# First cross attention of a perceiver block: the context turned by VectorE in 32x32 blocks, six batches ahead, and carried by the DMA of the probabilities

## The reference, cut to what matters

```python
xn, ln_lat = layer_norm(ctx, g1, b1), layer_norm(layernorm(x), g2, b2)
q, kv = ln_lat @ Wq, concat([xn, ln_lat], axis=1) @ Wkv      # 16 heads of 64
w = softmax(where(mask, einsum('bhld,bhnd->bhln', q * s, k * s), neg))
x = x + einsum('bhln,bhnd->bhld', w, v) @ Wout
```

## Time and profile before

| | |
|---|---|
| median of three runs | 2055.35 us (2054.4 to 2057.96) |
| the profiled execution | 2053.8 us, span 2051.7 us |
| busy, share of the span | PE 84%, DVE 78%, ACT 73%, POOL 44% |
| hardware DMA queue | 194678 packets, 256.53 MB, 50.0% of 16 engines |
| mean granted TensorE clock | 0.914 of full speed |

### The profile page before, as it was taken

The page is one execution under the profiler, slowest core; times in us unless marked ns, Lnnn a source line. Parts: engine busy times, 40 slices in busy tenths (PEclk is TensorE's granted clock), DMA queues, the critical chain, the costliest instruction groups (busy, mean ns, idle before and its releaser), DMA issues. The chain is left out here.

```text
span 2051.7 us, 51500 instructions
## 1 busy us (share of the span) xinstructions
PE 1718.3 (84%) x13455; PEld 1392.9 (68%) x13455; DVE 1594.6 (78%) x4998; ACT 1504.4 (73%) x4156; POOL 908.9 (44%) x1339
## 2 busy tenths in 40 slices
PE   3599999999999999971710679999999799749997
PEld 3489999999999999941500356666667566427775
DVE  4798888888888888837788669999999588636664
ACT  3488888888888888854765479999999588545553
POOL 1544444444444444304156034444444377335554
PEclk8599999999999999995755799999999799879998
DMA  4277676777777777610000059999999300103322
GB/s 139 85 167 165 160 160 157 161 163 162 159 162 163 159 160 164 151 42 0 0 0 0 2 147 250 252 250 251 249 249 248 73 1 0 32 13 102 91 87 82
DMA packets 196234, 259.54 MB, mean 127 GB/s; under 512 B 25136, under 2 KB 141328, under 8 KB 196032
## 3 DMA queue, kind: packets, MB, share of 16 engines
q1 hardware_dynamic: 194678, 256.53, 50.0%
q10 hardware_dynamic: 1194, 1.58, 0.3%
q0 software_dynamic: 288, 0.56, 0.1%
HBM read 86.09 MB, written 4.72 MB: 44 GB/s over the span
## 5 line engine op out<-in xcount | busy, mean ns | idle before, releaser
L778 ACT ACTIVATE a_prob<-a_neg,a_nmax 128x289 f32<-128x289 f32 x512 | 266.6, 525 | 1.4 <-DVE a_nmax L705 1.1
L840 PE MATMUL a_out<-a_probT,a_xn 128*128 128x256 f32 x1024 | 263.0, 380 | 5.0 <-DMA a_probT<-a_blocks 4.2
L1710 ACT ACTIVATE b_prob<-b_neg,b_nmax 128x257 f32<-128x257 f32 x512 | 260.6, 515 | 6.9 <-DVE b_nmax L1661 6.8
L671 POOL TENSOR_TENSOR a_xn<-a_z,g 128x256 f32<-128x256 f32 x128 | 93.8, 733 | 384.6 <-DVE a_z L739 384.6
L830 PE MATMUL a_score<-a_xnT,a_qT 128*128 128x290 f32 x1536 | 252.9, 314 | 2.5 <-DVE a_qT L750 2.5
L705 DVE CUSTOM_DVE_ANT_0 a_neg<-a_score,a_bias 128x289 f32<-128x289 f32 x512 | 211.6, 458 | 41.2 <-PE a_score L830 36.8
L786 ACT ACTIVATE a_prob<-a_prob,a_rinv 128x289 f32<-128x289 f32 x512 | 231.3, 527 | 1.8 <-DVE a_rinv L755 1.7
L830 PEld LDWEIGHTS a_score<-a_xnT,a_qT 128*128 128x128 f32 x1536 | 222.3, 190 | 9.6 <-issue 3.3
L1661 DVE CUSTOM_DVE_ANT_0 b_neg<-b_score,b_bias 128x257 f32<-128x257 f32 x512 | 188.6, 419 | 30.5 <-PE b_score L1801 15.3
L840 PEld LDWEIGHTS a_out<-a_probT,a_xn 128*128 128x128 f32 x1024 | 175.2, 191 | 19.8 <-DMA a_probT<-a_blocks 5.3
L716 DVE STREAM_TRANSPOSE a_blocks<-a_prob 128x1024 f32<-128x1024 f32 x128 | 159.4, 1245 | 24.0 <-ACT a_prob L786 17.7
(11 more groups left out here) (478 smaller groups left out, 4567.9 us busy)
## 6 DMA issues: line engine op xcount, KB each, us to landing
a_probT<-a_blocks SPq DMA_DIRECT2D x512, 192.0 KB, 3.6
b_probT<-b_blocks SPq DMA_DIRECT2D x256, 256.0 KB, 4.6
a_raw<-in_ctx SPq DMA_DIRECT2D x128, 128.0 KB, 2.9
b_raw<-in_ctx SPq DMA_DIRECT2D x64, 256.0 KB, 4.7
m_wide<-expert_weights SPq DMA_DIRECT2D x128, 128.0 KB, 2.9
a_kept<-keep SPq DMA_DIRECT2D x32, 257.0 KB, 3.4
b_kept<-keep SPq DMA_DIRECT2D x32, 257.0 KB, 4.8
b_v_rows<-ctx_tail_values SPq DMA_DIRECT2D x32, 256.0 KB, 4.7
```

The costliest lines, as they stand in the source:

```text
L778: nc.scalar.activation(prob[:, par, grp, 0:KEYS0], neg[:, grp, :], ACT.Exp, bias=nmax[:, par, grp:grp + 1], scale=-1.0, accum_out=rsum[:, ...
L840: nc.tensor.matmul(out_ps[:, half, 0:2 * P], xn[:, j, kt, :], probT[:, u, 2 * half:2 * half + 2, kt, :], start=(kt == 0), stop=False)
L1710: nc.scalar.activation(prob[:, (j + 5) % 4, grp, :], neg[:, par, grp, :], ACT.Exp, bias=nmax[:, par, grp:grp + 1], scale=-1.0, accum_out=r ...
```

## The change

The context is no longer transposed by TensorE through PSUM. VectorE turns the normalised context of batch s + 6 in 32x32 blocks into 64 more columns of `blocks`; the four DMAs of the step carry 448 columns instead of 384 and so put it, by features, next to the probabilities. Two steps later (batch s + 4) ScalarE copies it out of `probT` as the high half, and GpSimd subtracts for the low half. The pipeline begins with step -8 instead of -7, and 16 batches instead of 8 lie outside the loop. On TensorE the first values move ahead of queries and projection; on VectorE the statistics go first and the residual add ahead of the queries; ScalarE puts the query copy between exponentials 2 and 3; the projection has a bank of its own; z is written straight into `xn`.

```diff
-        z = sb("a_z", [P, 2, 2, D])
-        blocks = sb("a_blocks", [P, 2, KEY_STEP, KEY_TILES, GROUPS, L])
-        probT = sb("a_probT", [P, 2, 4, KEY_TILES, P])
+        blocks = sb("a_blocks", [P, 2, KEY_STEP, KEY_TILES * P + 2 * L])
+        probT = sb("a_probT", [P, 2, 4, KEY_TILES * P + 2 * L])
-        proj_ps = ctx_ps[:, 2 * P:2 * P + D]
+        proj_ps = proj_bank[:, 0:D]
-        LEAD, LAG = 7, 1
+        LEAD, LAG, REST = 8, 1, 16
-            return (g * 4 + (j // 2 + 1)) * 64
+            return (g * 4 + (j // 2 + 3)) * 64
+        def carried_ctx(j):
+            return probT[:, j % 2, :, KEY_TILES * P:].rearrange("p i (k m) -> p k i m", k=2 * KEY_STEP)
+        def ctx_cols(j, half):
+            return xnT[:, half, (j + 4) % 8, 0:2 * P].rearrange("p (k i m) -> p k i m", k=2 * KEY_STEP, i=4)
...
                 def spread_prob(g, j):
-                    wait_apart(k, sp, blocks_ready, s + 3)
+                    wait_apart(k, sp, blocks_ready, s + 7)
+                    if live(g, j, 4):
+                        wait_apart(k, sp, xnT_ready, s + 5)
...
-                        heads = slice(i * L, (i + 1) * L)
-                        sp.dma_start(probT[:, n, i].rearrange("p t q -> p (t q)"),
-                                     blocks[heads, n].rearrange("c r t g l -> c r (t g l)")).then_inc(probT_loaded[n], 16)
+                        sp.dma_start(probT[:, n, i], blocks[i * L:(i + 1) * L, n]).then_inc(probT_loaded[n], 16)
...
-                    if live(g, j, 8):
-                        if live(g, j, 4):
-                            wait_apart(k, sp, z_ready, s + 5)
-                        load_raw(g + 1, j)
+                    if live(g, j, 9):
+                        if live(g, j, 5):
+                            wait_apart(k, sp, z_ready, s + 6)
+                        load_raw(s + 9, j + 1)
...
             def _(pool):
+                    if live(g, j, 4):
+                        wait_apart(k, pool, xnT_hi, s + 5)
+                        nc.gpsimd.tensor_tensor(ctx_cols(j, LO), carried_ctx(j), ctx_cols(j, HI), ALU.subtract).then_inc(xnT_ready, 1)
...
             def _(dve):
-                    if live(g, j, 0):
+                    if live(g, j, 4) or live(g, j, 2):
...
+                    if live(g, j, 6):
+                        dve.wait_ge(xn_ready, s + 7)
+                        last = nc.vector.transpose(blocks[:, n, :, KEY_TILES * P:].rearrange("p f (r t m) -> p t f m r", r=KEY_STEP, t=2),
+                                                   xn[:, (j + 6) % 8].rearrange("p t (c f) -> p t f c", f=KEY_STEP))
+                    if live(g, j, 2):
+                        dve.wait_ge(prob_ready, s + 3)
+                        nc.vector.transpose(blocks[:, n, 0:2, 2 * P:3 * P].rearrange("p r (g l) -> p g r l", l=L),
+                                            prob[:, n, :, 2 * P:2 * P + 2 * L].rearrange("p g (r c) -> p g r c", c=L))
+                        last = nc.vector.transpose(blocks[:, n, :, 0:2 * P].rearrange("p r (t g l) -> p g r t l", t=2, l=L),
+                                                   prob[:, n, :, 0:2 * P].rearrange("p g (r t c) -> p g r t c", t=2, c=L))
+                    last.then_inc(blocks_ready, 1)
...
+                        wait(dve, out_ready, s)
+                        dve.wait_ge(rstd_ready, s + 8)
...
-                    if live(g, j, 5):
-                        dve.wait_ge(xnT_hi, s + 6)
-                        n = (j + 5) % 8
-                        nc.vector.tensor_tensor(xnT[:, LO, n, 0:2 * P], ctx_ps[:, 0:2 * P], xnT[:, HI, n, 0:2 * P],
-                                                ALU.subtract).then_inc(xnT_ready, 1)
...
+                    if live(g, j, 4):
+                        act.wait_ge(probT_loaded[j % 2], probT_loads(g, j))
+                        nc.scalar.activation(ctx_cols(j, HI), carried_ctx(j), ACT.Copy).then_inc(xnT_hi, 1)
...
-                    if live(g, j, 3):
-                        for grp in range(GROUPS):
-                            exp(g, j, grp)
+                    exps(g, j, (0, 1))
...
-                    if live(g, j, 5):
-                        act.wait_ge(ctx_turned, s + 6)
-                        nc.scalar.activation(xnT[:, HI, (j + 5) % 8, 0:2 * P], ctx_ps[:, 0:2 * P], ACT.Copy).then_inc(xnT_hi, 1)
+                    exps(g, j, (2, 3))
...
+                    if here:
+                        values(g, j, 0)
...
-                        wait(pe, xnT_ready, s + 5 if live(g, j, 4) else B)
+                        wait(pe, x_added, t - 1)
...
-                        values(g, j, 0)
-                    if live(g, j, 5):
-                        n = (j + 5) % 8
-                        pe.wait_ge(xn_ready, s + 6)
-                        wait(pe, xnT_ready, s + 5)
-                        if b == 0:
-                            wait(pe, x_added, t)
-                        for kt in range(2):
-                            last = nc.tensor.transpose(key_order(ctx_ps[:, 0:2 * P], kt), xn[:, n, kt, :], k.ident[:])
-                        last.then_inc(ctx_turned, 1)
```

## The result

The changed kernel takes 2124.59 us (median of four runs, 2121.12 to 2131.56) against 2056.65 us (four runs, 2054.4 to 2058.51) for the kernel before in the same session: a ratio of 1.0335, interval 1.0305 to 1.0365. It is slower by 68 us, beyond the range and beyond all three rivals' times. The profiled execution took 2131.56 us, with a span of 2129.8, against 2053.8 for the one before.

The account below looks back on a forecast made before the run. TensorE, never pausing, was taken as the bound at 24.86 us a tile. -13.5 over 30 tiles and +2.5 outside the body make -11.0: 2053.8 becomes 2042.8, 2044 for the median; range 2031 to 2060, the forecast's own 2037 to 2050.

Parts of the forecast that it names:

- the stall of the first values: TensorE waits for landed blocks at the first values, wanted 0.89 us earlier: 0.07 us in step 2, 0.08 later.
- The raw and mask loads stay behind the same transfers.: SP's queue: raw and mask loads keep their place behind the step's four transfers; new waits are for things done earlier.
- Stalls: 0.43 a tile. Tile 24.41.: TensorE's stalls of 0.07, 0.28 and 0.08 us where longer transfers meet shorter steps; gain 0.45 a tile.
- TensorE's list without stalls, 23.98 a tile: TensorE loses two transposes, 0.22 us a step: a tile goes from 24.86 to 23.98 us.
- The last landing 6.6 us after the first issue: Four transfers a step, 224 KB instead of 192: 6.6 us, halfway in bytes between 6.0 and 7.2.
- VectorE's turn, taken at 0.33 to 0.40, upper bound 0.27 more: VectorE's new strided 128x256 turn: lower value taken; the upper adds nothing until about 0.5 us.
- ScalarE's copy 0.40: ScalarE's context copy, now from SBUF: 0.40 us against 0.37 from PSUM, 0.60 if its runs of 8 cost.
- GpSimd at nothing: GpSimd: one more 128x256 subtraction of 0.73 us, done well before the transfer that waits for it; no cost.
- Ramp and drain +2.5: Outside the body: 1.3 us more before the first scores, 1.2 more for the drain's larger transfers.
- A: Rival: the transfers stay hidden, 224 KB landing like 192 (6.0 us); 23.98 a tile, 2031 us; chance 0.18.
- B: Rival: ScalarE's copy takes 0.60 or VectorE's turn over 0.9 us; about 24.8 a tile, 2050 to 2058; chance 0.17.
- Rival C: Slower: the transfer loop through ScalarE's copy and normalise sets the pace; gain gone at 6.8, 2080 at 7.2; chance 0.15.

Follow-up runs that it names:

- the repaired one: version 10: the padded kernel with statistics, context copy, first values and first raw loads moved; 2044.29 us, and 2096.08 us without its 40 do-nothing instructions.
- 7: The padded kernel with VectorE's statistics behind the masks, aggregation behind the turns, and ScalarE's context copy behind the normalising: 2063.07 us, ratio 1.0035.
- 9: 7 with TensorE's first value matmuls moved back behind the queries and the projection: 2045.88 us, ratio 0.9952.
- version 10: 9 with the first four raw batches loaded at once ahead of the loop: 2044.29 us, ratio 0.9949.
- 8: The padded kernel with late statistics and VectorE's context turn in runs of 32 columns, context permuted: 2071.11 us, ratio 1.0062.
- padded kernel: The changed kernel with 40 do-nothing instructions put ahead of VectorE's loop: 2091.98 us, ratio 1.0177.
- 6: The padded kernel with late statistics and transfers of 384 columns only (192 KB), the context's carriage left out: 2040.68 us, ratio 0.9927.

## Why the prediction was wrong, point by point

Three steps of the prediction failed: a term that it put at nothing without a reason (where VectorE's loop lies; 32.6 to 51.8 us here), a wait that it called unchanged (the raw load; 23.6 us), and the stall of the first values, which it sized at 0.15 us a tile and which measured 0.57.

- **Left out: VectorE's code.** Every number of the prediction is about work and waits that the trace of before shows, and that trace shows no stop on issue in the loop. The change adds seven instructions ahead of VectorE's loop and four inside, and so moves it from 426 to 433, where it spans one block too many. Measured by removal: 32.6 us on the changed kernel, 51.8 on the repaired one, and 72.6 when put on the kernel before. That is 2.7, 4.3 and 5.6 us a jump back, less where other waits hide part of a stop. The 5.6 are more than the 4.5 for which VectorE itself stands still in a turn ((32.4 + 17.5) / 11); where the rest arises was not taken apart. In the repaired kernel the loop's place alone turns a gain of 11.2 us into a loss (2096.08 against 2055.48).
- **"The raw and mask loads stay behind the same transfers."** True, and not followed up. The change puts the statistics first on VectorE's list, so what waits for the raw load is now ahead of the masks, and they are ahead of everything. 58.3 us of waits and 23.6 us of time. That statement was the place to ask who waits for them now.
- **"Stalls: 0.43 a tile. Tile 24.41."** The mechanism was right, the size too small. With the two causes above removed the tile takes 24.77 (786.5 us for 127 steps), so stalls of 0.79. Of these 0.12 are ScalarE's copy ahead of the normalising (7), for which the prediction had 0.28, and 0.57 the first values' new place (9), for which it had 0.15: 0.07 in step 2 and 0.08 in step 0. It wrote that moving them "costs no work, but they are wanted 0.89 us earlier", and by its sum the landing came just in time. That sum makes a round of 6.6 for the landing and 3.67 from the first values to the next issue (5.10 - 1.81 + 0.38), 10.27 against 10.20. In 7, in the 25 plain rounds that end in such a wait, the medians are 6.75, 0.04 until TensorE starts, and 3.78: 10.57, and TensorE's step 2 takes 5.47 instead of 5.10. So with next to no margin 0.15 and 0.11 us too little in two terms made the stall five times as long.
- **TensorE's list without stalls, 23.98 a tile:** right. 24.03 in version 10, 23.92 with 192 KB.
- **The last landing 6.6 us after the first issue:** near. Over all rounds in 200 to 800 us the median is 6.7 in each kernel with 224 KB, and 6.0 with 192 KB, as before. In the changed kernel one transfer of 224 KB lands a median of 4.2 us after its issue. But the prediction itself said that each 0.1 us is paid twice a tile.
- **VectorE's turn, taken at 0.33 to 0.40, upper bound 0.27 more:** the upper bound is right, 653 against 406 ns, and that it adds nothing is right too (8). The rule quoted in the prediction from the Trainium skill, page "SBUF — State Buffer", section "Door 1: The DMA port swizzle", is borne out in kind: with runs of 32 columns the same turn takes 428 ns. Which of the two strides costs, the read's or the write's, was not taken apart.
- **ScalarE's copy 0.40:** 0.412. GpSimd at nothing: no wait for its subtraction stands in the list.
- **Ramp and drain +2.5:** the drain is +0.4 instead of +1.2; the ramp is +9.0 instead of +1.3 (+7.4 in the padded kernel, whose first large turn starts at 102.42). One landing of 6.6 was put in the place of TensorE's transposes, but each of the first batches goes through the same chain of transfers, and the raw loads queue behind them. Loading four of them at once (10) brought the first large turn 2.0 us forward; that the chain of transfers is the rest was argued and not tested.
- **Rivals A and B:** 192 KB in place of 224 shows what hidden transfers would give: with the two first causes mended it is 2040.7, not 2031. Its tile of 23.92 us is the one that A forecast. B's conditions (a turn over 0.9, a copy of 0.6) were not met.
- **Rival C,** "the transfer loop sets the pace", named the right part and the wrong gate. Its condition was a landing of 6.8 or more; the landing was 6.7, and its route through ScalarE's normalising was worth 5 us. The loop that counts goes landing, first to last values, release of the buffer, next issue. That it is the transfers, 6 shows: 27.7 us for 32 KB less a transfer.

One repair after the other, from 2124.6 the loop's place takes 32.6, the statistics 23.6, the copy 5.4, the values' place 17.2, the raw loads 1.6, and 2044.3 are left. These are differences of successive kernels, so that they add up proves nothing, and each depends on the order: the loop's place is worth 51.8 at the end, the values' place 15.0 directly on the padded kernel. 2044 is near what the change is worth once these five things are mended. That it is the forecast to the digit is luck. In the profiled executions the layer became 15.2 us shorter and not 11.0: the steps take 21.4 us less where 14 were forecast, ramp and drain 6.1 more where it was 2.5. The unchanged layers behind it took 5.5 us more, which is their spread from run to run.

Open: where the last 0.2 us of the step with the projection goes (8.84 against 8.68), and more buffers for the turned probabilities, which by the account above would loosen the loop altogether, were not tried.

## What to carry to other kernels

After a change to a long loop, look in the profile for waits on "issue" that come once per jump back (the branch from the loop's end to its start) and for more packets on the instruction queue, whatever their share; some do-nothing instructions ahead of the loop tell at once whether it is the loop's place. When a change reorders an engine's list, ask of the instruction that is now first what it waits for; and of each double buffer how long it is held from its first reader to its last, since work that is put between them lengthens a loop that no engine's busy time shows.

## What the runs showed of the hardware that had not been expected

- 12 instructions that do nothing made a kernel of 2054 us slower by 72.6 us, and 40 of them by 2.8. Where the loop begins decided it: in the bad places each jump back stopped VectorE for up to 4.3 us at once and for a mean of 0.8 to 1.6 us more later in the turn, and five packets of 8.2 KB more went over the instruction queue.
- A 32x32 block turn of 128x256 that reads each fourth and writes each sixteenth element takes 653 ns; in runs of 32 it takes 406 to 428.
- 32 partitions to 128 in SBUF, four transfers behind each other: medians of 3.6 us from issue to landing for 192 KB and 4.1 to 4.2 for 224 KB, and 6.0 and 6.7 us from the first issue to the last landing.
